# VectorE's order at the begin of a batch: inner tile, residual sum, and where the scatter is waited for

## The reference, cut to what matters

```
xn = layernorm(x)
s  = attention(xn)                        # causal, 16 heads of 16
g  = silu((silu(xn Wg) * (xn Wu)) Wd)     # hidden size 768
x1 = x + s * g                            # the residual's sum
xn2 = layernorm(x1)                       # 1/sqrt(v + eps): "the second power"
out = x1 + hyena(xn2) * silu(top2_experts(xn2))
```

## Time and profile before

| | us |
|---|---|
| median of 3 runs | 1037.38 (1035.58 to 1037.94) |
| the profiled execution | 1044.48 |
| its span | 1042.7 |
| PE busy | 947.3 (91%) |
| DVE busy | 684.2 (66%) |
| ACT busy | 466.9 (45%) |
| POOL busy | 327.7 (31%) |
| granted TensorE clock, mean | 0.965 |

### The profile page before, as it was taken

How to read it: one execution, slowest core, us unless ns; L and a number is a source line. 1 busy time by engine, 2 the same in 40 slices (tenths; PEclk the granted TensorE clock), 3 DMA queues, 4 the chain that set the end, 5 groups by cost and what they waited for, 6 DMA issues and landing times.

```text
span 1042.7 us, 18970 instructions
## 1 busy us (share of the span) xinstructions
PE 947.3 (91%) x5860; PEld 717.7 (69%) x5860; DVE 684.2 (66%) x1451; ACT 466.9 (45%) x871; POOL 327.7 (31%) x605
## 2 busy tenths in 40 slices
PE   8789999999999999999999999867989985999996
PEld 6666866766776776775775766656656674888885
DVE  6474676576577477577577457453665326999998
ACT  4346456456446455455545536441222223443341
POOL 5223224514513613613613523602000063322320
PEclk9899999999999999999999989977999996999999
DMA  7956756346446435534544620457777552434421
GB/s 275 112 151 87 183 143 86 90 161 85 101 146 90 111 141 84 121 141 71 104 151 64 134 82 3 154 180 234 226 230 218 176 167 63 150 121 137 141 86 41
DMA packets 88187, 136.70 MB, mean 131 GB/s; under 512 B 9987, under 2 KB 63939, under 8 KB 86084
## 3 DMA queue, kind: packets, MB, share of 16 engines
q1 hardware_dynamic: 69636, 100.75, 40.2%
q0 software_dynamic: 6144, 16.79, 5.3%
q10 hardware_dynamic: 12352, 18.48, 5.1%
HBM read 79.36 MB, written 55.57 MB: 129 GB/s over the span
## 4 chain that ended last, share of the span: by engine, by line
PE 38%; issue 30%; POOL 13%; DVE 8%; ACT 2%; DMA 2%; SPq 1%; another core or an unknown queue 1%; POOLq 0%; DVEq 0%; ACTq 0%
PE PS L2028 6%; POOL PT L1851 6%; PE PS L317 4%; PE PS L340 4%; PE PS L373 4%; PE PS L1068 3%; PE PS L1054 3%; POOL slots_in L664 3%; PE PS L1026 3%; POOL h L1834 3%; PE PS L829 2%; PE PS L408 2%; POOL idle_p L1845 2%; PE PS L2011 1%; DMA xb<-slots_in 1%
## 5 line engine op out<-in xcount | busy, mean ns | idle before, releaser
L1563 DVE TENSOR_REDUCE Mneg<-PS 128x2 f32<-128x1024 f32 (+2 forms) x192 | 194.9, 1043 | 62.6 <-PE PS L1030 61.4
L1318 ACT ACTIVATE PT<-PS 128x512 f32<-128x512 f32 (+1 forms) x384 | 172.4, 530 | 111.7 <-PE PS L1054 109.9
L1026 PE MATMUL PS<-ks,qs 96*128 96x256 f32 (+3 forms) x512 | 118.7, 341 | 3.2 <-issue 2.1
L1054 PE MATMUL PS<-qs,ks 96*128 96x512 f32 (+3 forms) x512 | 118.6, 349 | 2.7 <-ACT PT L1318 1.5
L1845 POOL TENSOR_TENSOR idle_p<-neghalf 128x1 f32<-128x1 f32 x128 | 25.2, 197 | 299.5 <-ACT PT L1318 299.5
L829 PE MATMUL PS<-xnT,Wgu 128*128 128x512 f32 x384 | 103.4, 410 | 10.7 <-DVE h L1506 10.7
L1054 PEld LDWEIGHTS PS<-qs,ks 96*128 96x128 f32 x512 | 85.5, 188 | 37.5 <-ACT PT L1318 19.1
L2028 PE MATMUL PS<-Wes,xbT 128*128 x336 | 96.3, 397 | 4.8 <-issue 3.9
L1851 POOL TENSOR_SCALAR_AFFINE_SELECT PT<-PT 128x256 f32<-128x256 f32 x256 | 99.0, 410 | 0.0
L829 PEld LDWEIGHTS PS<-xnT,Wgu 128*128 128x128 f32 x384 | 69.9, 191 | 33.9 <-DVE h L1506 14.1
L1068 PE MATMUL PS<-PT,V 128*32 128x512 f32 (+3 forms) x1024 | 85.5, 440 | 4.6 <-POOL PT L1851 3.5
(11 more groups left out here) (241 smaller groups left out, 1609.5 us busy)
## 6 DMA issues: line engine op xcount, KB each, us to landing
qs<-qk_parts SPq DMA_DIRECT2D x96, 128.0 KB
ks<-qk_parts SPq DMA_DIRECT2D x96, 128.0 KB
slots_out<-yb ACTq DMA_DIRECT2D x28, 384.0 KB, 3.3
xb<-slots_in SPq DMA_DIRECT2D x83, 128.0 KB, 2.5
qk_parts<-qhl SPq DMA_DIRECT2D x16, 512.0 KB, 2.7
qk_parts<-khl SPq DMA_DIRECT2D x16, 512.0 KB, 3.1
xn2T_parts<-xn2T SPq DMA_DIRECT2D x8, 1024.0 KB, 4.9
xT<-xn2T_parts ACTq DMA_DIRECT2D x7, 1024.0 KB
```

Source lines behind the costliest of these rows:

```text
L1026: pe.matmul(out, qs[:, hd, P * qt:P * qt + P], ks[:, hd, 0:keys], start=n % a_bank == 0, stop=False, skip_group_check=True)
L1054: last = pe.matmul(PS[:, 4 + n, col:col + T - P * kt], ks[:, hd, P * kt:P * kt + P], qs[:, hd, P * kt:T], start=True, stop=True)
L1318: act.activation(PT[:, g % 2, j, 512 * n:512 * n + width], PS[:, 4 + n, 0:width], ACT.Exp, scale=SCALE).then_inc(S["exped"], 1)
L1563: dve.tensor_reduce(out=Mneg[:, 0, qt, heads[0]:heads[-1] + 1], in_=all_of, op=ALU.max, axis=AX.X, negate=True).then_inc(S["maxed"], 1)
```

## The change

Five edits. On DVE the residual's sum becomes a function of its own and moves out of `residual(b)`, across the end of the batch, to behind the next batch's `gated(3)`. The wait for the scatter moves from the end of a batch to directly ahead of `norm_rows` of the next; the count awaited there is that of the same scatter. The last batch keeps it at its end. Since the wait is not wanted in batch 1, that batch is written out in DVE's program and the loop runs over b = 2 to 5. On POOL `power` of the second layernorm moves ahead of the low part of tile 4.

```diff
--- before.py
+++ after.py
@@ -1660,6 +1660,8 @@
                     dve.wait_ge(S["g_sb"], 2 * b + n + 1)
                     part = G[:, 2 * n:2 * n + 2, :].rearrange("p t e -> p (t e)")
                     dve.tensor_tensor(part, PS[:, 2 + n, :], part, ALU.mult).then_inc(S["y_sb"], 1)
+
+            def residual_sum(b):
                 dve.wait_ge(S["y_sb"], 2 * (b + 1))
                 dve.wait_ge(S["xres_in"], 16 * (b + 1))
                 dve.tensor_tensor(xres[:, :, :], xres[:, :, :], G[:, :, :], ALU.add).then_inc(S["x1_sb"], 1)
@@ -1685,9 +1687,10 @@
                         last = dve.bn_stats(st[:, t, :], xres[:, t, :])
                 last.then_inc(S[var_sem], 1)
 
-            def sequence(b, first=False, last=False, ahead=True):
+            def sequence(b, first=False, second=False, last=False, ahead=True):
                 gated(b, 3)
                 if not first:
+                    residual_sum(b - 1)
                     norm_stats(b - 1, NORM_X1)
                 gated(b, 4)
                 if not first:
@@ -1695,6 +1698,8 @@
                 gated(b, 5)
                 last_hidden_low(b)
                 if not first:
+                    if not second:
+                        dve.wait_ge(S["sent"], 128 * (b - 1))
                     norm_rows(b - 1, NORM_X1)
                 if not last:
                     split_x(b + 1)
@@ -1714,7 +1719,6 @@
                     residual(b)
                 else:
                     residual_halves(b)
-                if not first:
                     dve.wait_ge(S["sent"], 128 * b)
 
             def spectrum_first():
@@ -1808,7 +1812,8 @@
             dve.tensor_scalar(first_row[:, :], ramp[:, 0:NE], float(CAP), None, ALU.mult)
             dve.tensor_scalar(next_row[:, :], ramp[:, 0:NE], float(CAP), None, ALU.mult)
             sequence(0, first=True)
-            with dve.Fori(1, B - 2) as b:
+            sequence(1, second=True)
+            with dve.Fori(2, B - 2) as b:
                 sequence(b)
             sequence(B - 2, ahead=False)
             sequence(B - 1, last=True, ahead=False)
@@ -1854,9 +1859,9 @@
 
             def sequence(b, first=False, last=False, ahead=True):
                 hidden_low(b, 3)
-                hidden_low(b, 4)
                 if not first:
                     power(b - 1, veps2, rstd2, "ln2_var", "ln2_std")
+                hidden_low(b, 4)
                 if last:
                     pool.wait_ge(t_hi, 1)
                     pool.tensor_tensor(Fwd[:, LO, :, :], st_f[:, :, :], f(Fwd[:, HI, :, :]), ALU.subtract
```

## The result

The changed kernel is slower: 1043.75 us median of 13 runs (1036.73 to 1055.59) against 1036.76 us (1031.64 to 1042.26, 13 runs) of the kernel before; ratio 1.0058, interval 1.0036 to 1.0080, or 6.0 us. The direction was forecast, the size was not: 2.8 us were forecast, and 1043.75 lies above the range's 1042.4. The ratio goes by fast runs alone and leaves out the one of 1055.59 us, whose granted clock was the lowest, 0.951. The profiled execution of the changed kernel has a span of 1040.8 us, less than the 1042.7 of before.

What follows compares the result with a forecast made beforehand. With TensorE busy 91% of the span, the bound taken was the chain through gated(4) to the route transposes. 3.06 - 0.25 gave +2.8 us on the median, 1040.2 us; range 1036.6 to 1042.4.

Steps and rivals of the forecast that it cites:

- The chain goes through gated(4), not gated(3): At batch boundaries, VectorE's gating of tile 4 sets when the route transposes start; in the loop 0.32 us later.
- Tile 5's wait: TensorE's 0.95 us idle ahead of inner tile 5; forecast gone; as rival bound 4.8 us faster, chance 0.12.
- The sum's move, loop boundaries, 5 x 0.32 = 1.60: VectorE, five loop boundaries: sum behind gated(3) makes gated(4) 0.32 us later each, 1.60 in all; bounds 0 to 4.5.
- A new order can't make them shorter; it can open gaps: VectorE's sum, gated(3) and statistics up to gated(4) keep 1.23, 0.59 and 1.45 us; only waits between can grow.
- Batch 0 to 1, 0.81: First boundary: gated(3) waits for silu 3, so gated(4) comes 0.81 us later.
- Batch 6 to 7, 0.65: Last boundary: gated(3) waits for silu 3, so gated(4) comes 0.65 us later.
- The sum against the profiled execution: All seven boundaries: gated(4) delays of 1.60 + 0.65 + 0.81 = 3.06 us together.
- Power ahead: GpSimd's power ahead of low part 4: delay hidden by 0.2 us; taken 0, bounds 0 to 0.3 x 7.
- Batch 1 written out: VectorE's batch 1 outside the loop: shorter, taken -0.25 us, bounds -0.42 to 0.1.
- The scatter's wait: Wait moved ahead of norm_rows: already met in both places; taken 0, bounds -0.1 to 0.
- The rival of the two low parts: VectorE's low part 5 waits for GpSimd's low part 4: 0.23 us a batch, 1.6 in all, 1041.8; chance 0.13.

Runs made afterwards that it cites:

- e2: Kernel before with only batch 1 written out in VectorE's program, loop over 2 to 5; 1035.86 us, ratio 0.9981 to the kernel before.
- e7: Kernel before, unchanged, one more execution with a profile; its seven routes sum to 99.6 us after the projection's start.
- e3: Kernel before with only the residual's sum moved behind gated(3); 1045.47 us, ratio 1.0057 to the kernel before.
- e12: Changed kernel with only the sum back at its old place behind the products; 1035.68 us, ratio 0.9975 to the kernel before.
- e11: Kernel before with all batches written out in VectorE's program; 1033.15 us, ratio 0.9953 to the kernel before.
- e8: Kernel before with GpSimd's low part of tile 2 ahead of a batch's last two scatter DMAs; 1056.82 us, ratio 1.0199.
- e9: Changed kernel with GpSimd's low part of tile 2 ahead of the last two scatter DMAs; 1040.32 us, ratio 1.0024 to the kernel before.

## Why the prediction was wrong

- **The chain goes through gated(4), not gated(3)**: right. Tile 5's wait went, and the time grew; the idle time moved behind tile 5 (forecast about 1.2 us, found 1.05).
- **The sum's move, loop boundaries, 5 x 0.32 = 1.60**: the step that failed, in "A new order can't make them shorter; it can open gaps", with the gap's size. The forecast anchored the old order at a second product 5.51 us after the projection and found silu 3 done 0.12 us after that product, so hardly any cover seemed lost. That anchor is not fixed. The product starts at +4.0, +4.7 or +5.5, while silu 3 starts at +5.6 to +5.8 in nearly all. In the old order the sum stands in the gap between the two. (With the product at +4.0 it runs beside the low part of tile 2 and takes 1.8 us, so gated(3) is hardly earlier than with +4.7: +6.5 beside +6.6 to +6.7.) In the new one the product is early throughout (+4.2 at the latest), but gated(3) hangs on silu 3 alone, so in the loop gated(4) is always at +9.5 to +9.8, instead of +8.4 to +8.8 behind an early product or +9.4 to +9.6 behind a late one. For an early boundary the cost is about 1.0 us, not 0.32; for a late one it is about 0.1. The sign of this was in the earlier trace rows: 2.89 us of idle time before the product put down to "remote", though by TensorE's own row the projection, begun at 350.84, was through at 350.84 + 3.61 = 354.45. Another was the 7.1 us by which the profiled execution was above the median. The clock does not explain them: it was 0.965 there, and 0.963 in the mean of the 103 later runs.
- **Batch 0 to 1, 0.81**: gated(4) at +8.66 instead of +7.83, 0.83. **Batch 6 to 7, 0.65**: +9.46 instead of +8.93, 0.53. Both right in size. Here gated(4) is nearly the same in the two executions of the kernel before (+7.83 in both; +8.93 and +8.88), so the anchor did no harm.
- **The sum against the profiled execution**: 3.06 forecast, 2.5 found in the table. The two ends have 1.5 of it, as forecast (0.81 + 0.65); the five loop boundaries have 1.0 and not 1.60, since the new order came out better than its sum: gated(4) at +9.56 where the forecast had 360.67 - 350.84 = +9.83. Silu 3 started 0.15 us earlier, the statistics 0.04 after the sum and not 0.12, gated(4) 1.32 after the statistics' start and not 1.45, while gated(3) came 0.21 after silu 3 and not 0.12. So against its own execution the loop term was too large, and against others too small. What was off was to carry it over to the median. The bounds given for this term, 0 to 4.5, did not hold the 5.3 either, since they asked how slow the new order might be and not how fast the old one might be in other executions.
- **Power ahead**: taken 0, +0.1 at equal clock with an error of 1.2; 0.1 us a batch in the traces.
- **Batch 1 written out**: -0.25, found -0.4 at equal clock with an error of 1.2. In the traces the stretch from route transposes to heads' transposes, which the forecast asked about, is 58.88 us in the changed kernel, against 59.39 and 59.21 in the two executions before: -0.5 and -0.3. What the written-out program gives at batch 0 to 1 (e2 has gated(4) at +7.45 there and not +7.83) comes on top.
- **The scatter's wait**: taken 0, from batch 3 to 4. That is right for the old order there. At batch 6 to 7 the wait is not always met: it ended gated(3)'s idle time in e7 (0.16 us) and in e3 (2.21 us). In the time, e12 against e2 shows no difference beyond the errors.
- **The rival of the two low parts**: they do meet, and the mechanism is there; the size is 0.1 us a batch and not 0.23. Low part 5 started at 368.31 beside low part 4 (367.26 to 368.54) and took 0.79 us instead of 0.69. The same shows in other pairs, and each time the one that started second is longer by the overlap less 0.13 or 0.14 us: low part 5 by 0.10 for 0.23 us of overlap; low part 3 beside the sum (362.40 to 363.61) by 0.25 for 0.38; the sum beside low part 2 by 0.57 for 0.71 (e12, rows above) and by 1.17 for 1.30 (e11). That is what one would see if the second got no data through until the first was done, and had 0.13 us of its own start to overlap. The rule of the Trainium skill, "SBUF — State Buffer", "Who interferes with whom", has this pair share an exclusive lock, in which the one that is issued second blocks fully. The trace agrees; power, which reads only 4 columns, stretched nothing (low part 5 took 0.69 us beside it).

## What to carry to other kernels

Before a wait is removed by a swap, ask what the old order hid: an instruction that stands ahead of a gate and looks like its delay may be filling a wait that has to be sat out anyway. The order that keeps it there can be improved by taking away what draws it out, here GpSimd's low part beside it. A gap that one execution shows five times alike can still be on one of several levels; where an idle time is put down to something the trace can't name, take a second execution's value as a bound, for the kernel before as well. A wait at the end of a loop body stands ahead of the next iteration's first instruction: moved to its real user, it costs nothing here, and lets the producer run later.

## What was not expected of the hardware

- With the scatter on GpSimd, silu 3 starts at +5.6 to +5.8 in nearly every case, although TensorE's rows have its input ready by about +4.3 (358.67 - 355.41 in the rows after, and four more matmuls at 5.98 / 24), and without the scatter, in batch 0 to 1, at +4.75. At most boundaries in the loop it starts within 0.25 us after the end of the low part of tile 2 (+5.5 to +5.7). But at batch 6 to 7 it can start ahead of that end (+5.59 and +5.69 in the changed kernel), and once, in e11 at batch 1 to 2, it started at +5.00 with the end at +5.68. With the low part ahead of the last two scatter DMAs it starts at +4.73. So the place of the low part matters, and its end is not simply what is waited for. What holds silu 3 is not shown: in e8 and e9 that low part runs at +1.9 to +3.15 and the first product, which falls into that time, is not late.
- A VectorE instruction with two SBUF inputs and one of GpSimd cost each other their overlap less about 0.13 us. It falls on whichever of the two started second, here 0.1 to 1.2 us (not beside power, which reads 4 columns).
- A loop on VectorE costs more than its own instructions: from one batch's route transposes to the next it takes 79.0 us in batches 1 to 5 with all of them written out, and 79.5 to 80.7 in the loop (the two executions of the kernel before).
